# A vision tower on one core: quantised activations held as float16 integers plus 1536, the first embeddings by chunks, centring on ScalarE, weight passes on GpSimd, and new sequences on five engines

## The reference, cut to what matters

```
h = einsum(patches(x), W) + b
a = h @ w1.T + b1 ; a = dynamic_conv(a, softmax(a @ ww.T + bw)) ; a = a @ w2.T + b2
h = layernorm(h + layernorm(h + a) * gamma + beta)
act_quant(x)    : s = 127 / max(max|x|, 1e-5);      round(x * s) / s           # per token
weight_quant(w) : s = 1 / max(mean|w|, 1e-5);       clip(round(w * s), -1, 1) / s
bitlinear(x, w) = act_quant(x) @ weight_quant(w).T
h = layernorm(h + bitlinear(silu(bitlinear(h, w_gate)) * bitlinear(h, w_up), w_down))
```

## Time and profile before

| | |
|---|---|
| median of 3 runs | 127.66 us (127.19 to 128.3) |
| the profiled execution's own time | 127.84 us |
| its span in the trace | 125.4 us |
| PE busy | 112.0 us (89%) |
| VectorE busy | 92.7 us (74%) |
| GpSimd busy | 71.3 us (57%) |
| ScalarE busy | 65.2 us (52%) |
| bytes moved by DMA | 12.44 MB |

### The profile page before, as it was taken

The page is one execution under the profiler, slowest core; times in us unless marked ns, Lnnn a source line. Parts: engine busy times, 40 slices in busy tenths (PEclk is TensorE's granted clock), DMA queues, the critical chain, the costliest instruction groups (busy, mean ns, idle before and its releaser), DMA issues.

```text
span 125.4 us, 2349 instructions
## 1 busy us (share of the span) xinstructions
PE 112.0 (89%) x722; PEld 72.2 (58%) x722; DVE 92.7 (74%) x240; ACT 65.2 (52%) x110; POOL 71.3 (57%) x123
## 2 busy tenths in 40 slices
PE   6999989999899999999999999999999984897600
PEld 2377456688358568555855677476676652663400
DVE  5029764387438929999998998996999989699740
ACT  0402139865030834856775469568554775686300
POOL 7990000209002488722886247498978488998870
PEclk9999999999999999999999999999999999999995
DMA  4999999932231011313330220222320001101112
GB/s 91 394 322 408 423 418 423 404 89 19 56 31 10 0 48 14 29 47 33 61 35 6 52 26 3 55 25 57 33 51 5 0 0 42 42 0 42 47 43 82
DMA packets 22313, 12.44 MB, mean 99 GB/s; under 512 B 18013, under 2 KB 20317, under 8 KB 21918
## 3 DMA queue, kind: packets, MB, share of 16 engines
q1 hardware_dynamic: 21504, 10.72, 29.8%
q10 hardware_dynamic: 798, 1.58, 3.9%
HBM read 9.95 MB, written 2.34 MB: 98 GB/s over the span
## 4 chain that ended last, share of the span: by engine, by line
POOL 23%; DVE 13%; PE 12%; issue 8%; ACT 2%; POOLq 1%; DVEq 0%; ACTq 0%
POOL gu L1031 6%; POOL rstd L969 6%; PE bank L400 3%; PE bank L383 3%; POOL f L1038 2%; POOL veps L968 2%; POOL res L1009 2%; PE bank L322 2%; DVE a L734 2%; POOL h L1018 2%; DVE sc L788 1%; POOL shift_out L1007 1%; DVE gu L782 1%; POOL h1b L1026 1%; DVE stats L740 1%
## 5 line engine op out<-in xcount | busy, mean ns | idle before, releaser
L322 PE MATMUL bank<-xT,tokW 128*128 128x256 f32 x96 | 22.8, 387 | 0.3 <-DMA tokW<-in_tokW 0.2
L322 PEld LDWEIGHTS bank<-xT,tokW 128*128 128x128 f32 x96 | 18.3, 194 | 4.7 <-DMA tokW<-in_tokW 1.6
L997 POOL TENSOR_TENSOR taps<-probs,inv_total 128x256 f32<-128x256 f32 x8 | 6.8, 854 | 21.0 <-DVE inv_total L709 21.0
L968 POOL TENSOR_SCALAR veps<-mv 128x1 f32<-128x1 f32 x24 | 5.0, 210 | 22.1 <-DVE mv L719 14.5
L400 PE MATMUL bank<-conv_w,vpad 128*32 128x128 f32 x256 | 15.7, 397 | 0.4 <-DMA conv_w<-shear 0.4
L969 POOL TENSOR_TENSOR rstd<-veps,minus_half 128x1 f32<-128x1 f32 x24 | 14.4, 599 | 2.0
L383 PE MATMUL bank<-wl,h1T 128*128 128x496 f32 x32 | 14.6, 579 | 0.0
L630 ACT ACTIVATE q2T<-bank,minus_magic 128x512 bf16<-128x512 f32 x15 | 10.3, 688 | 5.8 <-PE bank L493 5.7
L493 PE MATMUL bank<-ident,gu 128*128 128x128 f32 x64 | 9.6, 275 | 3.6 <-POOL gu L1031 2.2
L617 ACT ACTIVATE silu<-bank,sc 128x512 f32<-128x512 f32 x16 | 11.0, 687 | 2.7 <-PE bank L453 2.7
L400 PEld LDWEIGHTS bank<-conv_w,vpad 128*32 128x32 f32 x256 | 8.5, 122 | 6.6 <-DMA conv_w<-shear 1.7
(11 more groups left out here) (110 smaller groups left out, 231.1 us busy)
## 6 DMA issues: line engine op xcount, KB each, us to landing
xT<-in_xT SPq DMA_DIRECT2D x3, 768.0 KB, 16.1
w_raw<-in_wg SPq DMA_DIRECT2D x1, 1024.0 KB, 12.6
w_raw<-in_wu SPq DMA_DIRECT2D x1, 1024.0 KB, 14.6
w_raw<-in_wd SPq DMA_DIRECT2D x1, 1024.0 KB, 16.5
shear<-taps SPq DMA_DIRECT2D x8, 128.0 KB, 1.9
conv_w<-shear SPq DMA_DIRECT2D x64, 16.0 KB, 1.9
out_dram<-res SPq DMA_DIRECT2D x8, 128.0 KB
xT<-in_xT ACTq DMA_DIRECT2D x2, 384.0 KB, 5.5
```

Source lines behind the costliest of these rows:

```text
L322: last = nc.tensor.matmul(ps_embed(pair, m), tokW[:, k, m * P:(m + 1) * P], xT[:, pair, k, :], start=(k == 0), stop=(k == KC_PATCH - 1))
```

## The change

It does seven things.

1. Quantised activations are `round(x * scale) + 1536` in float16 (STEP) in place of float32 plus MAGIC. Between 1024 and 2048 float16 has steps of one, so writing the sum rounds it. The transposes of them are float16 in and float16 out, with a float16 identity, and the eight transposes of an inner tile share one bank, so that `out_q2T` takes both halves in one instruction over 1024 columns. The quantised weights are float16 too. `silus` writes into `gu` and `inner` multiplies it there; the quantised values have a tile of their own, `q2`.
2. The first pair of tiles is embedded chunk by chunk: embedding weights and tokens come in six transfers each, on SyncE's and ScalarE's queue, and both halves of the output advance with every chunk. The warm-up has six products, not ten. w1o moves from SyncE's queue to ScalarE's, and w2 ahead of the norm rows.
3. `centre` moves from VectorE to ScalarE and negates its result; the scales are negated to match.
4. The scales: `mid_scales` has two instructions and `out_scales` one where there were five; `inner_scales` two and `down_scale` one where there were four. `inv_std_mid` on GpSimd has a third small instruction and its power covers two columns; a new `inner_limit` is one small instruction per tile on GpSimd.
5. All three passes after the sum, for the gate and the down matrix, are on GpSimd (six passes; before, three); VectorE keeps only the clip of the up matrix.
6. The three-part bias is written by four instructions over all 65 rows, not six, with a mask; the bias products take 65 rows and not 128.
7. The lists of PE, ScalarE, VectorE and GpSimd are written anew. ScalarE loads its table of functions four times, not six.

```diff
-WARM_UP = 10
+WARM_UP = 6
+STEP = 1536.0
-            sp.dma_start(tokW[:, 0:3, :], tokW_d[:, 0:3, :]).then_inc(tokW_in[0], 16)
-            sp.dma_start(tokW[:, 3:6, :], tokW_d[:, 3:6, :]).then_inc(tokW_in[1], 16)
-            sp.dma_start(w1o[:], w1o_d).then_inc(w1o_in, 16)
+            for k in range(KC_PATCH):
+                sp.dma_start(tokW[:, k, :], tokW_d[:, k, :]).then_inc(tokW_in[k], 16)
...
+            def first_embeds():
+                for k in range(KC_PATCH):
+                    pe.wait_ge(tokW_in[k], 16)
+                    pe.wait_ge(x0_in[k], 16)
+                    for m in range(KC):
+                        last = nc.tensor.matmul(ps_embed(0, m), tokW[:, k, m * P:(m + 1) * P], xT[:, 0, k, :],
+                                                start=(k == 0), stop=(k == KC_PATCH - 1))
+                        if k == KC_PATCH - 1:
+                            last.then_inc(embed_ps, 1)
...
-                    last = nc.tensor.transpose(ps_q1T[:, k, :], q1[:, k * P:(k + 1) * P], ident[:])
+                    last = nc.tensor.transpose(ps_q1T[:, k, :], q1[:, t % 2, k * P:(k + 1) * P], ident16[:])
...
                     last = nc.tensor.transpose(ps_q2T(t, half)[:, k * P:(k + 1) * P],
-                                               gu[:, t % 2, half, k * P:(k + 1) * P], ident[:])
+                                               q2[:, t % 2, half * HALF + k * P:half * HALF + (k + 1) * P], ident16[:])
...
+            first_embeds(); logit_bias(); logit_weights(); values(0); embed(1, 0); logits(0); embed(1, 1)
+            logits(1); weight_means(0, 2); embed(2, 0); logits(2); embed(2, 1); logits(3); residual(0); conv(0)
...
+            project_out(7); gate(5, 0); up(5, 0); inner_transposes(3, 0); inner_transposes(3, 1); up(5, 1)
+            gate(5, 1); in_transposes(6); down(3, 0); down(3, 1); gate(6, 0); up(6, 0); inner_transposes(4, 0)
+            inner_transposes(4, 1); up(6, 1); gate(6, 1); down(4, 0); down(4, 1); in_transposes(7)
+            inner_transposes(5, 0); inner_transposes(5, 1); gate(7, 0); up(7, 0); up(7, 1); gate(7, 1)
...
+            def centre(t):                                      # on ScalarE
+                act.wait_ge(var_mid, t + 1)
+                if t >= 2:
+                    act.wait_ge(h3_ok, t - 1)
+                nc.scalar.activation(centred[:, t % 2, :], a2[:, t % 2, :], ACT.Identity, bias=mv[:, 1, t % 2, 0:1],
+                                     scale=-1.0).then_inc(centred_ok, 1)
...
+                at["limit", t] = mark(nc.vector.tensor_scalar(s[:, 1:2], s[:, 0:1], -1.0 / 127.0, s[:, 11:12],
+                                                              ALU.mult, ALU.min))
+                after(at["limit", t])
+                nc.vector.reciprocal(s[:, 7:8], s[:, 1:2]).then_inc(q1_scale_ok, 1)
...
+            def inner_limit(t):                                 # on GpSimd
+                pool.wait_ge(q1_scale_ok, t + 1)
...
+                nc.gpsimd.tensor_scalar(sc[:, t % 4, 10:11], sc[:, t % 4, 7:8], rstd[:, 1, t % 2, 1:2], inner_min[:, 0:1],
+                                        ALU.mult, ALU.mult).then_inc(inner_min_ok, 1)
...
+            normalise(0); weight_round(0); weight_clip(0); normalise(1); weight_finish(0, wq_gate_ok)
+            inv_std_attn(0); normalise(2); add_beta(0); normalise(3); inv_std_mid(0); add_beta(1)
+            inv_std_attn(1); inv_std_mid(1); normalise(4); add_beta(2); weight_round(2); inner_limit(0)
...
+            inner_limit(5); scale_h3(5); inner_limit(6); add_h3(3); inv_std_mid(7); scale_h3(6)
+            quant_inner(5, 0); quant_inner(5, 1); result(2); inner_limit(7); add_h3(4); scale_h3(7)
+            quant_inner(6, 0); quant_inner(6, 1); inv_std_out(3); result(3); add_h3(5); inv_std_out(4)
+            result(4); add_h3(6); inv_std_out(5); result(5); inv_std_out(6); result(6); inv_std_out(7)
```

More of the change, by code:

```diff
@@ L82, in vit_tower @@
         magic = sb("magic", [P, 1])
+        minus_step = sb("minus_step", [P, 1])
+        step = sb("step", [P, 1])
+        halves = sb("halves", [P, 2])
         abs_sum = sb("abs_sum", [P, 3])
@@ L520, in _ @@
                 nc.tensor.matmul(bank[7][:, :], ones_bf[:], ones_bf[:, 0:1].broadcast_to([P, 512]), start=True, stop=True)
-            embed(0, 0); embed(0, 1); logit_bias(); logit_weights(); values(0); residual(0); logits(0)
-            embed(1, 0); weight_means(0, 2); logits(1); embed(1, 1); values(1); embed(2, 0); logits(2); conv(0)
-            logits(3); project_out(0); weight_means(2, 3); embed(2, 1); residual(1); conv(1); logits(4)
-            project_out(1); embed(3, 0); in_transposes(0); values(2); gate(0, 0); up(0, 0); values(3)
@@ L525, in _ @@
-            residual(2); up(0, 1); gate(0, 1); conv(2); logits(5); in_transposes(1); project_out(2); gate(1, 0)
-            up(1, 0); values(4); residual(3); embed(3, 1); up(1, 1); gate(1, 1); conv(3); logits(6)
-            project_out(3); inner_transposes(0, 0); in_transposes(2); logits(7); inner_transposes(0, 1); conv(4)
-            residual(4); down(0, 0); down(0, 1); project_out(4); gate(2, 0); up(2, 0); in_transposes(3)
-            values(5); residual(5); up(2, 1); gate(2, 1); conv(5); gate(3, 0); up(3, 0); project_out(5)
@@ new lines, in _ @@
+            logits(1); weight_means(0, 2); embed(2, 0); logits(2); embed(2, 1); logits(3); residual(0); conv(0)
+            values(1); project_out(0); logits(4); residual(1); conv(1); values(2); weight_means(2, 3)
+            project_out(1); embed(3, 0); in_transposes(0); logits(5); residual(2); conv(2); gate(0, 0); up(0, 0)
+            project_out(2); values(3); up(0, 1); gate(0, 1); in_transposes(1); embed(3, 1); gate(1, 0); up(1, 0)
+            residual(3); up(1, 1); gate(1, 1); conv(3); logits(6); in_transposes(2); project_out(3); gate(2, 0)
@@ new lines, in _ @@
+            up(2, 0); values(4); up(2, 1); gate(2, 1); logits(7); inner_transposes(0, 0); inner_transposes(0, 1)
+            residual(4); conv(4); down(0, 0); down(0, 1); project_out(4); in_transposes(3); values(5)
+            gate(3, 0); up(3, 0); conv(5); residual(5); up(3, 1); gate(3, 1); values(6); project_out(5)
+            inner_transposes(1, 0); inner_transposes(1, 1); conv(6); residual(6); down(1, 0); down(1, 1)
+            project_out(6); in_transposes(4); values(7); gate(4, 0); up(4, 0); residual(7); up(4, 1); gate(4, 1)
@@ L817, in last_scales @@
[L817 to L824 removed]
+                after(at["first", LAST])
@@ L1060, in _ @@
+            nc.gpsimd.tensor_copy(ident16[:], ident[:]).then_inc(const_ok, 1)
             nc.gpsimd.memset(conv_w[:], 0.0).then_inc(pool_zeros_ok, 1)
-            normalise(0); normalise(1); add_beta(0); inv_std_attn(0); inv_std_mid(0); normalise(2)
-            weight_finish(0, wclip_gate, wq_gate_ok); add_beta(1); inv_std_attn(1); weight_round(2)
-            inv_std_mid(1); normalise(3); normalise(4); add_beta(2); inv_std_attn(2); scale_h3(0)
-            quant_inner(0, 0); scale_h3(1); add_beta(3); inv_std_mid(2); scale_h3(2); quant_inner(0, 1)
@@ L1065, in _ @@
-            weight_finish(2, wclip_down, wq_down_ok); normalise(5); inv_std_attn(3); inv_std_mid(3); add_beta(4)
-            add_h3(0); inv_std_attn(4); normalise(6); inv_std_mid(4); normalise(7); quant_inner(1, 0)
-            add_beta(5); quant_inner(1, 1); scale_h3(3); inv_std_out(0); inv_std_attn(5); quant_inner(2, 0)
-            inv_std_mid(5); add_h3(1); result(0); add_beta(6); scale_h3(4); quant_inner(2, 1); inv_std_attn(6)
-            quant_inner(3, 0); quant_inner(3, 1); inv_std_out(1); inv_std_mid(6); add_beta(7); add_h3(2)
@@ new lines, in _ @@
+            inv_std_attn(0); normalise(2); add_beta(0); normalise(3); inv_std_mid(0); add_beta(1)
+            inv_std_attn(1); inv_std_mid(1); normalise(4); add_beta(2); weight_round(2); inner_limit(0)
+            inv_std_attn(2); inner_limit(1); scale_h3(0); inv_std_mid(2); weight_clip(2); add_beta(3)
+            quant_inner(0, 0); normalise(5); scale_h3(1); inner_limit(2); quant_inner(0, 1); inv_std_attn(3)
+            weight_finish(2, wq_down_ok); scale_h3(2); inv_std_mid(3); normalise(6); quant_inner(1, 0)
@@ new lines, in _ @@
+            add_beta(4); add_h3(0); inv_std_attn(4); inner_limit(3); quant_inner(1, 1); inv_std_out(0)
+            inv_std_mid(4); result(0); normalise(7); add_beta(5); quant_inner(2, 0); inv_std_attn(5)
+            scale_h3(3); quant_inner(2, 1); add_beta(6); inv_std_mid(5); add_h3(1); scale_h3(4); inv_std_attn(6)
+            quant_inner(3, 0); inv_std_out(1); inner_limit(4); quant_inner(3, 1); add_beta(7); inv_std_mid(6)
+            result(1); add_h3(2); quant_inner(4, 0); inv_std_attn(7); inv_std_out(2); quant_inner(4, 1)
```

413 lines of the change are left out of this document (213 added, 200 removed).

## The result

The changed kernel takes **127.0 us** (median of 20 executions, 126.53 to 128.3) against 127.68 for the kernel before beside it on the same chip (20 executions): ratio 0.9952, 95% interval 0.9932 to 0.9973. It is faster, by half a per cent, where 122.9 was predicted; the prediction had counted everything within one per cent, above 126.4, as no change. The profiled execution took 127.6 us, its span 125.7; the span is 0.3 longer than in the profiled execution of before, and what lies outside it 0.5 shorter (1.9 and not 2.44), so that the traces show the end 0.3 later while the medians show it 0.7 earlier. The traces explain why hardly any of the predicted 4.9 us came; they can't explain a difference of half a microsecond.

The account below looks back on a forecast made before the run. PE's product start distances bound the kernel up to the last convolution, a GpSimd queue the last 27 us. Lead 1.3 + 0.7 + 0.8 = 2.8 us at `conv(7)`; 127.84 - 4.9 = 122.9 us, range 119.5 to 127.2.

Parts of the forecast that it names:

- predicted 4.9 us: At the end: last GpSimd power at 117.0, not 121.91, taking the profiled execution from 127.84 to 122.9 us.
- Head: Chunked loads and shorter warm-up: last embedding start at 10.3, not 11.6, a gain of 1.3 us (0 to 2.9).
- the risk that the prediction named: At the start: bias columns, late near 9, covered until 10.3; if later, the first product after the embeddings is late.
- Body: Up to `conv(7)`: 0.7 us of short PE waits gone, 0.8 from transposes; with 1.3 before, a lead of 2.8.
- at half the distance of the float32 ones: PE's float16 inner transposes, if only columns count: 0.055 us each; 0.3 to 1.65 us by `conv(7)`, 0.8 taken.
- Rival (b): Lead handed back by PE waits before `conv(7)`, which starts at 94.3 again; 126.1 us, chance 0.22.
- Tail: After `conv(7)`: tile 7's statistics at 95.4, GpSimd's list to 107.2, then 9.8 us more; last power ends 117.0.
- three signs of being wrong: PE waits for taps at `conv(2)` or `conv(7)`; two-column power over 0.9 us; last power waits for VectorE.
- its sign for the tail: GpSimd without pause behind `quant_inner(6, 1)`, which ends near 107; last power starts at once after the one before.
- a GpSimd queue, with PE idle beside it: Reading of the kernel before: what the last 27 us are, GpSimd running without a pause from 111.85.
- Rival (c): GpSimd's queue bounds from near 66 us on, with 6.6 us more work against 2.8 of lead; 131.6 us, chance 0.13.
- less bound: VectorE loses 3.8 us of centring, some 3.7 of weight passes and clips, and two or three 0.2 us instructions a tile.

Follow-up runs that it names:

- experiment 5: Changed kernel with the old head: ten warm-up products, halves instead of chunks, w1o on SyncE's queue; 127.29 us, ratio 0.9976.
- Experiment 10: Kernel before, with eight more small GpSimd instructions (2.2 us) in the middle norms of tiles 4 to 7; 129.46 us, ratio 1.0133.
- experiment 3: Changed kernel with the third GpSimd instruction of `inv_std_mid` issued three times for tiles 4 to 7, not once; 128.85 us, ratio 1.0089.
- experiment 2: Changed kernel with `inner_limit` and the third instruction of `inv_std_mid` moved to VectorE, the power covering one column again; 125.84 us, ratio 0.9815.
- version 7: Changed kernel with seven results, the inner limits and the third middle-norm instruction on VectorE, and three output buffers; 123.36 us, ratio 0.9676.
- experiment 6: Kernel before, without the change, with its seven GpSimd results made by one VectorE instruction each; 128.89 us, ratio 1.0111.

## Why the prediction was wrong

**Head: small, and it hardly counts.** First product at 3.88 (4.0 to 4.6 predicted), the embeddings end near 10.2 as forecast, but the bias products start at 10.99 (10.3 predicted), 0.7 us early and not 1.3: they waited 0.77 us for a copy on VectorE that itself waited for the bias columns, the risk that the prediction named. `values(0)` starts at 16.46, 0.2 earlier than before, and with the old head `conv(7)` starts as early (experiment 5).

**Body: right in direction, and better than predicted.** `conv(7)` leads by 3.66 where 2.8 was predicted, with a head that gave nearly none of it. The transposes are at the low end of their price; the group in the kernel after:

```profile
L508 PE MATMUL bank<-ident,q 128*128 128x128 f16 x64 | 5.6, 224 | 2.4 <-POOL q L1080 1.4 <-ACT q L648 0.9
```

Eight of them take 0.61 us with a last one of 0.22, so 0.055 each, "at half the distance of the float32 ones". The prediction counted thirty ahead of `conv(7)`, 6 of the first kind; the trace has 34, with 10 of these (two a tile). That is 1.9 us and not the 0.8 taken. The Trainium skill (TensorE: Matmul & The Clock Gate, Part 2, Back-to-back issue gap) has some 81 ns for a load and a product of 128 columns; this trace has 55, and the measurement decides. Of the other 1.8 us of lead, PE's named waits between its first bias product and `conv(7)` are 0.7 (0.9 before, 0.2 now), as predicted; the rest of 1.1 is mostly the new order, with 0.2 at most from the head, and no run took it apart. Rival (b), a lead handed back in the body, is the nearest in time (126.1) and is not what happened: no wait for taps, `conv(7)` far ahead of 94.3. That 127.0 lies inside the stated range of 119.5 to 127.2 is luck, for only (b) reached so far up.

**Tail: the step that failed.** The prediction said "GpSimd's list is, after 0.7 us for the statistics (96.1): power and its partner for tile 7", as if GpSimd were free then. The data came on time, tile 7's first statistics at 95.22 where 95.4 was predicted; GpSimd took up that norm at 99.26, 3.2 us later than 96.1. From there to the last power's end the prediction had 20.9 us; it took 22.9, 2.0 more, mostly for the quantisation at 0.79 and not 0.68 a half, three limits at 0.34 on average and not 0.27, the wider power and its third instruction 1.36 and not 1.2, a partner instruction of 0.48, adds of 0.8 to 0.9, and a last stretch of 10.2 and not 9.8 (111.98 to 122.19). Together 5.2 us, from 117.0 to 122.19. The path of data to tile 7 was worked out, but not the queue of the engine that it ends in: counted from `inv_std_attn(6)`, a list of 28 us of old work and 3.5 of new was waiting. None of the prediction's three signs of being wrong appeared (no wait for taps, the wide power at 0.71, the last power not held by VectorE), and its sign for the tail, GpSimd without a pause behind `quant_inner(6, 1)`, was met while the forecast failed; only the time at which that ends, 111.90 and not near 107, gave the miss away. A queue without pauses says that it is the bound, not how long it is.

**What the reading of the kernel before had.** The prediction itself called the last 27 us "a GpSimd queue, with PE idle beside it". That is too strong: PE is busy 17.05 us of 20 from 93 to 113, and GpSimd still waits 1.58 us before 99.07. It then dropped the queue where it mattered, in the sum of the tail.

**The rival dismissed.** Rival (c), the GpSimd queue as bound "from `weight_finish(2)` on, near 66 us", was given 0.13 because "that idle time between 66 and 98 is about 10 us now". It is what happened, from about 77 us, at a smaller size: the added work ate the lead of PE instead of exceeding it, hence 127.0 and not 131.6. The argument against it was the wrong one: idle time of an engine whose waits hang on its own earlier work is no store of free time. Experiment 10 measures it: 2.2 us of new work into the kernel before cost 1.6. In experiment 3 it costs 1.85 of 2.2, in experiment 2 taking 16 instructions away gives back 1.16. That PE's lead was real and that GpSimd's queue kept it back is shown by experiments 2 and 7 together: with the queue relieved, 3.6 us come out, at 123.36. That this is 0.5 from the forecast is chance, for version 7 also takes from GpSimd seven results that were there before the change, and has a third buffer.

**VectorE** was rightly called less bound (15.0 us of 20 from 93 to 113, from 17.7), but nothing was drawn from that: the free time was there, while the small instructions went to the engine that had none.

**Open:** what share the new order has in PE's lead, what made the kernel of experiment 6 slower, and what bounds version 7 below 123 us beyond tile 7's own path.

## What to carry to other kernels

Before work is moved to an engine, add up that engine's queue from a common landmark to the end, in both versions, and compare the sums: a lead upstream shortens the kernel only by what this sum leaves of it. Do not count an engine's idle time as cover without asking what ends each wait; if that is a chain through the same engine, new work can cost most of its length (1.6 of 2.2 us here). A small instruction costs the distance to the next start, not its one element of work, so put it on the engine with slack, and test a suspected queue by adding and by removing a few instructions: the slope tells what share comes out at the end, and the sum from the landmark whether it is the queue.

## What the runs showed of the hardware

- GpSimd: an instruction on one number per partition takes 0.27 to 0.29 us start to start, with three operands 0.29 to 0.44; the power 0.55 us for one column and 0.71 for two. Writing float16 and not float32, a half of `quant_inner` takes 0.78 us to the next start and not 0.68. On VectorE the two new small instructions take 0.13 to 0.15 and 0.27 to 0.28.
- VectorE stopped beside GpSimd passes twice in the kernel after. VectorE first, then GpSimd's pass with which it overlaps:

```profile
52.99 1.44 DVE L805 TENSOR_SCALAR sc<-mean_neg,sc,rstd 128x2 f32<-128x2 f32 x1
...
69.02 1.61 DVE L768 SCALAR_TENSOR_TENSOR a<-a,rstd,h1b 128x256 f32<-128x256 f32 x1
```

```profile
52.43 1.98 POOL L1092 TENSOR_SCALAR w_raw<-w_raw,w_scale 128x2048 f32<-128x2048 f32 x1
...
68.47 1.90 POOL L1102 TENSOR_SCALAR w_q<-w_raw 128x2048 f16<-128x2048 f32 x1
```

  The small scale instruction, 0.27 us elsewhere, ended at 54.43, as the pass did at 54.41; the norm, 0.48 us for tile 7 at 100.12, at 70.63, 0.26 behind the pass. The Trainium skill (SBUF — State Buffer, Who interferes with whom) says that a VectorE instruction with two SBUF inputs and a GpSimd one that reads SBUF contend, and that the second fully blocks. The norm agrees but for 0.2 us: held to the end of the pass at 70.37 and then 0.48 long, it would have ended at 70.85. The two stalls cost 1.2 and 1.1 us of VectorE, and PE has no wait between them and `conv(7)`.
- The clock granted to PE fell to 1.2 GHz near 107 us in the kernel after, behind five waits of 0.80 to 1.45 us since 97; 2.4 GHz was back near 111. Eight down products take 1.03 us at the high level (clock 1.00, the kernel after at 114.00) and 2.02 at the low one (0.50, version 7 at 113.38).
